# Rounding and splitting of expert weights put into other steps of an attention and mixture-of-experts kernel

## What is computed

```python
# cut from the reference
x = x + tanh(g_xattn[0]) * xattn(ctx_2048, layernorm(x), mask, mask, ...)
#   k, v = split(ctx @ W_src.T + b_src) * mask;  q = (ln @ W_tgt.T + b_tgt) * mask
#   attn = softmax(where(mask == 0, -inf, q.k / sqrt(16)));  out = [ln, attn @ v] @ W_out.T + b_out
x = x + tanh(g_ffn[0]) * ffn(layernorm(x), ...)
#   scores = sigmoid(x @ gate.T + bias); the best 2 of 9, their scores divided by their sum -> cw
#   out += cw[:, e] * ((silu(x @ ew1[e].T) * (x @ ew3[e].T)) @ ew2[e].T)   for e in 0..8
```

## Time and profile before

| | us |
|---|---|
| median of 3 executions | 217.67 |
| lowest and highest | 217.46, 218.7 |
| span of the profiled execution | 234.1 |

### The profile page before, as it was taken

How to read it: one execution, slowest core, us unless ns; L and a number is a source line. 1 busy time by engine, 2 the same in 40 slices (tenths; PEclk the granted TensorE clock), 3 DMA queues, 4 the chain that set the end, 5 groups by cost and what they waited for, 6 DMA issues and landing times.

```text
span 234.1 us, 5788 instructions
## 1 busy us (share of the span) xinstructions
PE 205.4 (88%) x1606; PEld 166.9 (71%) x1606; DVE 149.6 (64%) x523; ACT 142.7 (61%) x399; POOL 128.8 (55%) x230
## 2 busy tenths in 40 slices
PE   8999986999999999898883946299999999999981
PEld 3577653666666676565573945299999999999881
DVE  0469997788898698897865822344443444456774
ACT  2286869988778876786471620266667666666210
POOL 4237745132325876786783578556675756557320
PEclk9999999999999999999998897589999999999998
DMA  5999999999910100011372221121222221261194
GB/s 164 368 377 242 407 381 409 408 370 318 342 55 13 36 23 26 23 36 38 86 214 62 61 76 49 41 53 55 61 69 68 52 65 47 49 218 53 37 348 163
DMA packets 23602, 34.91 MB, mean 149 GB/s; under 512 B 2562, under 2 KB 15879, under 8 KB 23443
## 3 DMA queue, kind: packets, MB, share of 16 engines
q1 hardware_dynamic: 20610, 29.27, 37.9%
q0 software_dynamic: 2240, 4.23, 5.5%
q10 hardware_dynamic: 720, 1.02, 1.5%
HBM read 15.85 MB, written 19.06 MB: 149 GB/s over the span
## 4 chain that ended last, share of the span: by engine, by line
PE 56%; DVE 14%; another core or an unknown queue 7%; ACT 6%; DMA 6%; issue 5%; POOL 4%; SPq 1%; POOLq 0%; DVEq 0%; ACTq 0%
PE pt_ps L1363 10%; PE score_ps L1321 5%; PE pt_ps L1372 4%; PE score_ps L1323 4%; PE score_ps L1322 4%; PE score_ps L1176 4%; DMA kheads<-y_rows 3%; PE pt_ps L1116 3%; PE ps_a L1226 3%; PE pt_ps L1214 3%; PE score_ps L1126 2%; PE ps_b L1283 2%; DVE less L827 2%; ACT probs L401 2%
## 5 line engine op out<-in xcount | busy, mean ns | idle before, releaser
L616 POOL DMA_INDIRECT y_rows<-vals,ids x38 | 37.8, 995 | 17.2 <-ACT vals L473 9.6
L1363 PE MATMUL pt_ps<-w,probsT 128*128 x234 | 34.4, 285 | 14.6 <-ACT probsT L480 6.7
L1363 PEld LDWEIGHTS pt_ps<-w,probsT 128*128 128x128 f32 x234 | 32.1, 198 | 15.9 <-issue 15.8
L593 POOL DMA_INDIRECT x_rows<-stage,slot x32 | 32.7, 1022 | 10.4 <-issue 7.7
L401 ACT ACTIVATE probs<-score_ps,less 128x128 f32<-128x128 f32 x128 | 37.9, 419 | 0.4 <-DVE less L827 0.4
L1043 DVE TENSOR_TENSOR xg_low<-ps_a,xg_high 128x128 fp32r<-128x128 f32 x40 | 11.7, 291 | 37.1 <-issue 23.6
L473 ACT ACTIVATE vals<-pt_ps,xg 128x128 f32<-128x128 f32 x38 | 14.0, 368 | 34.4 <-PE pt_ps L1363 24.7
L1321 PE MATMUL score_ps<-w_high,xg_low 128*128 x80 | 30.3, 379 | 0.0
L1051 DVE TENSOR_TENSOR probs<-probs,score_ps 128x352 f32<-128x352 f32 x40 | 20.8, 521 | 11.2 <-PE score_ps L1323 5.3
L1323 PE MATMUL score_ps<-w_high,xg_high 128*128 x80 | 26.6, 332 | 0.0
L1322 PE MATMUL score_ps<-w_low,xg_high 128*128 x80 | 26.5, 332 | 0.0
(11 more groups left out here) (179 smaller groups left out, 445.6 us busy)
## 6 DMA issues: line engine op xcount, KB each, us to landing
x_rows<-pads SPq DMA_DIRECT2D x1, 9945.0 KB, 37.3
w_low<-in_w13T SPq DMA_DIRECT2D x3, 1056.0 KB, 11.0
xg<-x_rows SPq DMA_DIRECT2D x40, 65.0 KB
ctx_r<-in_ctxT SPq DMA_DIRECT2D x4, 512.0 KB, 7.7
y_rows<-pads SPq DMA_DIRECT2D x1, 2048.0 KB, 16.6
w<-in_w2T SPq DMA_DIRECT2D x1, 1728.0 KB, 11.2
kheads<-y_rows SPq DMA_DIRECT2D x3, 512.0 KB, 5.0
mask_b<-in_mask SPq DMA_DIRECT2D x4, 256.0 KB, 8.0
```

Source lines behind the costliest of these rows:

```text
L593: pool.indirect_dma_start(x_rows[:, :], bass.IndirectOffsetOnAxis(ap=slot[:, par, c, p:p + 1], axis=0), stage[:, par, c, p, :], None, boun ...
L616: pool.indirect_dma_start(y_rows[:, :], bass.IndirectOffsetOnAxis(ap=ids[:, s:s + 1], axis=0), yt[:, s, :], None, bounds_check=last_row, o ...
L1363: last = nc.tensor.matmul(into[:, 0:D], hidT[:, q3, c, :], w2[:, bass.ds(e3, 1), c, :].rearrange("p o d -> p (o d)"), start=(c == 0), stop ...
```

## The change

`high(4)` and `high(5)` go ahead of the wait for `kT` of pass 3, `high(6)`, `high(7)` and `high(8)` to the ends of steps 2, 3 and 4. `low(0)`, `low(1)` and `low(2)` stand in a row in step 1, `low(3)` to `low(7)` in steps 2 to 6 and `low(8)` in step 9. The number of instructions and their sizes stay. The whole of it:

```diff
+LOWS = {1: (0, 1, 2), 2: (3,), 3: (4,), 4: (5,), 5: (6,), 6: (7,), 9: (8,)}
@@ ACT, pass j
                 if j + 1 < NG:
                     norm(j + 1)
+                if j == NG - 1:
+                    high(4)
+                    high(5)
                 act.wait_ge(k_done, j + 2)
...
-                for e in ((), (0, 1), (2, 3), (4, 5, 6))[j]:
+                for e in ((), (0, 1), (2, 3), ())[j]:
                     high(e)
@@ ACT, step k
-                if k < 2:
-                    high(7 + k)
+                if 2 <= k < NE - 4:
+                    high(4 + k)
@@ DVE, pass j
-                if j >= 2:
-                    low(j - 2)
@@ DVE, step k
-                if 2 + k < NE:
-                    low(2 + k)
+                for expert in LOWS.get(k, ()):
+                    low(expert)
```

## The result

The changed kernel takes 215.02 us (median of 6 executions, 214.43 to 215.78), the kernel before, run beside it, 217.88 us; the ratio is 0.9865, with a 95% interval from 0.9842 to 0.9888. The mechanism of the forecast is there, a little larger than counted (1.95 us); a second one, worth about 1 us in the median, was not in it at all.

What follows compares the result with a forecast made beforehand. PE was taken as saturated from the third attention step, waiting before that while the pipeline fills. Gains 0.40 + 0.79 + 0.22 + 0.21 = 1.62 us, less 0.05 to 0.1, gave 1.55: 217.67 to 216.1 us, range 215.4 to 217.2.

Steps and rivals of the forecast that it cites:

- the likeliest case: The whole sum holds: 1.55 us gained, 216.1 us, with its own width 215.7 to 216.6; chance 0.62.
- What bounds: PE saturated from the third attention step on; before that the pipeline fills, engines take turns and PE waits.
- DVE at the end of the projections: Without `low(0)` ahead of `vals`, `qT` starts 0.40 us earlier; of its 1.88 us only 0.40 count.
- Ahead of the first maxima: Removing `low(1)` on DVE adds 0.79 us; first maxima of step 0 come 1.19 earlier, with 0.2 us cover.
- ACT ahead of `kheads`: Two casts fill ACT's 1.93 us of idle time there to the brim, pushing `kheads` perhaps 0.1 us, at no cost.
- ACT in steps 1 and 2: Casts `high(7)` and `high(8)` leave; PE's turning of heads then bounds the copies: further gains of 0.22 and 0.21 us.
- The three subtractions: In a row on DVE after the maxima of step 1: 2.66 us, hidden by a wait with 0.7 us left.
- The rival in which they block step 2: DVE and POOL lock each other out, 1.88 us per subtraction; all behind 0.65 late, 218.3 us; chance 0.03.
- Ordinary steps and step 9: Moved casts counted 0, at most 0.3 us in all; `low(8)` in step 9 counted 0.05 us lost.
- The full-rule sum: If the DVE and POOL lock holds in full, the three subtractions end at 39.9; gain 1.35 in place of 1.55.
- the sentence that a microsecond in that stretch counts as one in the runs: The stretch of the change holds no unnamed stalls, so the span's gain carries over one to one to 217.67.
- more than forecast: Rival: PE's turning of heads does not bound the copies, both casts count in full; 2.5 us, 215.1; chance 0.07.

Runs made afterwards that it cites:

- dve_only: The kernel before with only the subtractions on DVE moved, the casts on ACT left in place: 216.46 us, ratio 0.9923.
- the halves: The kernel before with only the subtractions moved (216.46 us, ratio 0.9923), and with only the casts moved (217.69 us, ratio 0.9962).
- single pieces: The changed kernel with one subtraction put back ahead of the first maxima (215.92 us), between maxima of steps 0 and 1 (215.16), or ahead with all casts back (217.07).
- a_later: The changed kernel with nine matmuls (1.95 us) put on PE ahead of the scores of step 0: 218.61 us, ratio 0.9972.
- one_back: The changed kernel with one subtraction back ahead of the first maxima, two left in step 1: 215.92 us, ratio 0.9922.
- the filled kernels: The kernel before with idle-filling PE matmuls: step 1 (ratios 1.0007, 0.998), also ahead of the scores (217.11 us), or also between attention and tiles (217.07 us).

## Why the prediction was wrong

The direction, the mechanism and the likeliest case were right; the size was half of what was measured.

1. *What bounds.* Right: from step 2 on the steps are the same (60.2 us in both), all of the gain lies ahead.
2. *DVE at the end of the projections*, 0.40: measured 0.36. *Ahead of the first maxima*, 1.19 in all: measured 1.30; the mask's bias on DVE holds it 0.14 us less as well (0.61 in place of 0.75 us), and the 0.2 us of cover that I left between it and the scores were not there.
3. *ACT ahead of `kheads`*: right, the two casts filled the hole (30.40 to 31.9) and cost nothing. That they had to leave their old place for the exponentials to gain more than 1.03 us, `dve_only` shows.
4. *ACT in steps 1 and 2*, a further 0.22 and 0.21, of 0.67 for each cast: measured 0.24 and 0.24 at the copies. The claim that PE's turning would then bound was right; the second copy waits 0.27 us for it. But I ended the sum at the copies. PE's own wait of 0.35 us ahead of the product with the values is gone as well: a further 0.16, 1.94 against the 1.62 of my sum. This is the term of the sum that was mis-sized.
5. *The three subtractions*: counted 2.66 with 0.7 us left, measured 2.69 with 0.59 left. The rival in which they block step 2 did not come.
6. *Ordinary steps and step 9*: counted 0.05 to 0.1, measured nil, made of +0.12 and +0.07 in steps 9 and 10 and -0.23 in step 12. POOL was held beside `low(8)`, by 0.59 us. The full-rule sum (1.35) was further off than the row's.
7. *The step that failed* is the sentence that a microsecond in that stretch counts as one in the runs and that the sum may be carried over one to one to 217.67. I read the clock as 1.00 in the ten microseconds of the earlier trace rows and put no rival on it. In about 80% of the executions of before (73 low and 5 lower still, of 98) the clock falls in the middle, in the profiles at one of two places and for a net price of 1.19 or 1.27 us; the median is that of such an execution. In the changed kernel it was 0 of 10. The gain in the median is 1.95 us of filling and 0.8 x 1.2 = 1.0 us of clock (an estimate from these shares and prices), together 2.9. The executions without a low clock agree: those of before average 217.2 us, the ten of the changed kernel 215.0, and only 2.2 of the 3.1 us between the averages of all executions remain. Nothing in that one profile showed the fall behind step 1, but two things in it could have warned me. An execution 16.4 us away from the median is a poor sample of it. And its page shows the clock falling behind the stalls in the tiles (slices 22 to 27), so that idle times of PE can cost more than their length:

```profile
PEclk9999999999999999999998897589999999999998
```

I also listed only PE's short waits, 0.38 and 0.35 us. The two longest of that stretch, 1.23 and 0.59 us in step 1, are among those that stand ahead of the fall where it comes:

```profile
36.85 0.66 PE L1214 MATMUL pt_ps<-fst,probs 128*128 128x128 f32 x4 [1.23 <-ACT probs L401]
...
39.13 0.82 PE L1226 MATMUL ps_a<-probsT,v_cur 128*32 128x128 f32 x16 [0.59 <-ACT probsT L411]
```

8. The rival *more than forecast* gave nearly the right time (215.1) for a wrong reason: the casts did not count in full. That is luck.

What is shown: where the 1.95 us arise, by the halves and single pieces; the two places of the fall (five profiles) and its price at each; that PE's 1.2 us of idle time in step 1 stand ahead of the first in all three. What is made likely: that the time at which the second stretch comes matters (`a_later`). What stays open is why some executions have a fall and others not: all three profiles with the fall behind step 1 had 1.2 and 0.4 us of idle time ahead of it and then 0.32 or 0.59, and so had `one_back`, without a fall, and the first profile of before; I have no pair of kernels that differ in this idle time alone and have enough executions; the filled kernels differ from before by less than the idle theory wanted, and some of their low executions have a place that no profile shows.

## What to carry to other kernels

Work without an early deadline costs where a pipeline fills and its engine is the one that the next waits for (a subtraction cost its full 0.8 us ahead of the first maxima, but only 0.36 of its 1.88 us ahead of `vals`), and nothing two steps later; look for it there first, and read the gain to the last engine in the row, not to the first that comes free. One profile is one execution: before a sum is carried over to a median, compare the profiled execution's mean clock and span with those of several others. A change that moves everything behind it by 2 us may win or lose a microsecond at a thin stretch of PE far behind it, so try a kernel's timing at two offsets before its last microsecond is put down to the edit.

## What the runs showed of the hardware that I had not expected

- The granted clock fell to half (1.2 GHz) for some 3 us behind idle times of PE no longer than 1.2 us each (1.23, 0.38 and 0.59 us in step 1; 0.59 and 0.43 us between attention and tiles), at a net price of 1.19 and 1.27 us.
- With the stretch between attention and tiles at 85 us from the reference event 8 of 12 executions had the low clock, with the same stretch at 83 us 0 of 10.
- The first 24 matmuls of PE took 6.79 to 8.14 us in the seventeen profiles, and in sixteen of them the reference event followed 15.7 us after the next matmul began: over a microsecond of the time is decided there.
- A subtraction of two SBUF operands on DVE held a POOL copy back by 0.59 us (0.90 in place of 0.31) of the 0.76 us that it had left.
- One profiled execution of before held 16.4 us of stalls that none of the sixteen others had.
